# Thirty edge-list transfers moved into the drain of each middle convolution, out of the groups of the relational pass

## The reference, cut to what matters

```python
x = _layernorm(x + _L0(x, edge_index, ...))        # five attention convolutions, 4 heads
x = _layernorm(x + _L1(x, edge_index, types, ...)) # relational attention, 4 edge types
x = _layernorm(x + _L2(x, edge_index, ...))        # two GCN layers over (src, dst)
x = _layernorm(x + _L3(x, src, dst, weight, ...))  # out[src] += weight * h[dst]
```

## Time and profile before

| | |
|---|---|
| median of 3 runs | 5815.96 us (5811.11 to 5824.28) |
| the profiled execution | 5819.82 us, of which its span 5817.9 us |
| busy: PE, DVE, ACT, POOL | 3599.2, 3391.6, 1515.3, 4067.9 us |
| granted clock of PE, mean of the span | 0.686 |
| DMA, mean over the span | 117 GB/s |
| chain that ended last | no engine or line with as much as 1% of the span |
| edge passes of the middle convolutions, from POOL's first to its last gather | 747.9 to 1280.5, 1376.2 to 1908.5, 2005.5 to 2537.8 us |
| relational edge pass, POOL's first gather to its last transfer | 3345.7 to 4113.9 us |

### The profile page before, as it was taken

One profiled execution on the slowest core, in us unless ns is written; L12 is line 12 of the kernel. 1 busy time (PEld: TensorE's weight loads), 2 busy tenths in 40 slices (PEclk: granted clock), 3 DMA queues, 4 the chain that ended last, 5 costly groups with the idle time before them and its releaser, 6 DMA issues. The chain is left out here.

```text
span 5817.9 us, 84345 instructions
## 1 busy us (share of the span) xinstructions
PE 3599.2 (62%) x17681; PEld 2904.7 (50%) x17903; DVE 3391.6 (58%) x9203; ACT 1515.3 (26%) x3581; POOL 4067.9 (70%) x4170
## 2 busy tenths in 40 slices
PE   5667766666676656675787556666644444446555
PEld 3556546654666456554565345656533333334334
DVE  7777756665666556665666366666444343336665
ACT  4334323432343333333454322222100010000000
POOL 4477577766777577757777677777577767766775
PEclk6777767867777777787898755555655555557877
DMA  7656365645565366636664342332122222212111
GB/s 236 171 170 184 84 205 171 189 124 165 170 184 166 106 192 181 175 87 202 174 181 120 88 86 65 67 73 46 38 53 52 53 62 53 52 48 57 52 52 51
DMA packets 632362, 681.70 MB, mean 117 GB/s; under 512 B 179026, under 2 KB 514488, under 8 KB 631800
## 3 DMA queue, kind: packets, MB, share of 16 engines
q0 software_dynamic: 166560, 384.79, 24.1%
q1 hardware_dynamic: 465496, 293.65, 17.6%
HBM read 620.51 MB, written 57.47 MB: 117 GB/s over the span
## 5 line engine op out<-in xcount | busy, mean ns | idle before, releaser
L616 POOL DMA_INDIRECT kvconv<-kv_tab,src_all x1664 | 1626.4, 977 | 648.7 <-issue 497.8
L616 POOL DMA_INDIRECT rowsg_<-h_tab,src_all x832 | 788.7, 948 | 319.8 <-issue 253.0
L630 POOL DMA_INDIRECT lst_tab<-pay,ord_now x416 | 428.3, 1029 | 315.8 <-issue 244.7
L616 POOL DMA_INDIRECT rowss_<-h_tab,dst_i_g x416 | 399.1, 959 | 160.4 <-issue 120.1
L616 POOL DMA_INDIRECT rows_r<-rel_tab,idx_r x416 | 412.6, 992 | 132.7 <-issue 125.0
L616 POOL DMA_INDIRECT kvlast<-kv_tab,src_all x416 | 409.9, 985 | 133.1 <-issue 122.2
L1057 ACT ACTIVATE Sconv<-s8conv 128x512 f32<-128x512 fp8e4 x384 | 240.7, 627 | 401.3 <-PE pA1conv L1015 286.4
L1119 DVE TENSOR_TENSOR msgconv<-kvconv,sm_attEconv 128x512 f32<-128x512 f32 x416 | 285.6, 687 | 78.3 <-PE pA0conv L1015 28.0
L1015 PEld LDWEIGHTS pA0conv<-Sconv,msgconv 128*128 128x128 f32 x1664 | 303.0, 256 | 13.4
L1015 PE MATMUL pA0conv<-Sconv,msgconv 128*128 128x128 f32 x1664 | 302.0, 342 | 10.6 <-issue 6.5
L1015 PEld LDWEIGHTS pA1conv<-Sconv,msgconv 128*128 128x128 f32 x1664 | 291.4, 247 | 17.0
(11 more groups left out here) (681 smaller groups left out, 8861.6 us busy)
## 6 DMA issues: line engine op xcount, KB each, us to landing
qwinconv<-q_tab SPq DMA_DIRECT2D x1664, 64.0 KB
kvconv<-kv_tab,src_all POOLq DMA_INDIRECT x1664
st8conv<-st_tab SPq DMA_DIRECT2D x52, 512.0 KB
s8conv<-s_tab SPq DMA_DIRECT2D x52, 512.0 KB
qwinlast<-q_tab SPq DMA_DIRECT2D x416, 64.0 KB
kv_tab<-stageconv_n SPq DMA_DIRECT2D x28, 512.0 KB, 3.2
rowsg_<-h_tab,src_all POOLq DMA_INDIRECT x832
rel_tab<-stage_r SPq DMA_DIRECT2D x28, 272.0 KB, 3.9
```

The costliest lines, as they stand in the source:

```text
L616: nc.gpsimd.indirect_dma_start(rows[:, par * TG + t, :], None, tab, bass.IndirectOffsetOnAxis(ap=idx[:, g * TG + t:g * TG + t + 1], axis=0 ...
L630: nc.gpsimd.indirect_dma_start(lst_tab, bass.IndirectOffsetOnAxis(ap=ord_now[:, i:i + 1], axis=0), pay[:, i, :], None).then_inc(sem("liste ...
```

## The change

The batch of a middle convolution grows from 34 to 64 columns. `fetch` loads all 64; POOL issues the first 30 behind the 416 gathers of that convolution's edge pass, and the other 34 in the joint as before, where it waits for the landing of all. In the relational pass two transfers follow each group in place of ten, all 26 from one load by SP, so that the load in mid-pass goes, and the last batch there grows from 40 to 54. Joint 0, the last convolution, the stage behind it and the projection stage keep theirs. The total stays 416.

```diff
@@ -37,8 +37,9 @@
 RW = D + 2 * H
 JOINT = 34
 DRAIN = 30
-EACH = 10
-LISTED = [(CONVS - 1) * JOINT, DRAIN + 32, 48, EACH * GROUPS, 40]
+PER = DRAIN + JOINT
+EACH = 2
+LISTED = [JOINT + 3 * PER, DRAIN + 32, 48, EACH * GROUPS, 54]
 MOST = 70
 assert sum(LISTED) == T
 NT = NPAD // P
@@ -762,8 +763,8 @@
                 def _(pool):
                     pool.wait_ge(sem("ord_in"), 32 * (l + 1))
                     settle(pool)
-                    list_rows(pool, JOINT)
-                    pool.wait_ge(sem("listed"), 16 * JOINT * (l + 1))
+                    list_rows(pool, JOINT, 0 if isinstance(l, int) else DRAIN)
+                    pool.wait_ge(sem("listed"), 16 * PER * l + 16 * JOINT)
                     settle(pool)
 
                 @block.sync
@@ -918,8 +919,10 @@
                 @block.gpsimd
                 def _(pool):
                     gather_all(pool, lambda g, par: gather_group(pool, tag, l, g, par, kv_tab, src_all, kv), since)
-                    if deg is not None:
-                        pool.wait_ge(sem("ord_in"), 32 * CONVS)
+                    if rank is None:
+                        pool.wait_ge(sem("ord_in"), 32 * (l + 1))
+                        if not isinstance(l, int):
+                            settle(pool)
                         list_rows(pool, DRAIN)
 
                 @block.sync
@@ -1369,7 +1372,7 @@
 
                 def fetch(sp):
                     if not first:
-                        order_in(sp, l * JOINT, JOINT)
+                        order_in(sp, l * PER - DRAIN, PER)
                     load_next(sp, l + 1, nx)
                     sp.dma_start(nx["ln"][:, :], col0[ds(l, 1), :, :].rearrange("l p n -> (l p) n")
                                  ).then_inc(sem("nx_cols"), 16)
@@ -1557,16 +1560,11 @@
                         gather_group(pool, tag, 0, g, par, rel_tab, idx1, rows)
                         if g == 0:
                             pool.wait_ge(sem("ord_in"), 32 * (CONVS + 2))
-                        if g == 6:
-                            pool.wait_ge(sem("ord_pool"), 32)
-                        list_rows(pool, EACH, EACH * (g if g < 6 else g - 6))
-                        if g == 5:
-                            pool.wait_ge(sem("listed"), 16 * (sum(LISTED[:3]) + 6 * EACH))
-                            order_in(pool, sum(LISTED[:3]) + 6 * EACH, 7 * EACH, "ord_pool")
+                        list_rows(pool, EACH, EACH * g)
                     gather_all(pool, group)
                     pool.wait_ge(sem("listed"), 16 * sum(LISTED[:4]))
                     order_in(pool, sum(LISTED[:4]), LISTED[4], "ord_pool")
-                    pool.wait_ge(sem("ord_pool"), 64)
+                    pool.wait_ge(sem("ord_pool"), 32)
                     list_rows(pool, LISTED[4])
                     pool.wait_ge(sem("listed"), 16 * T)
 
@@ -1599,7 +1597,7 @@
                                     settle(sp)
                                 scatter_rows(g + 1, 1 - par)
                     scatter_rows(0, 0)
-                    order_in(sp, sum(LISTED[:3]), 6 * EACH)
+                    order_in(sp, sum(LISTED[:3]), LISTED[3])
                     for g in range(3):
                         group(g, g % 2)
                     with sp.Fori(1, (GROUPS - 1) // 2 - 1) as k:
```

## The result

The changed kernel takes 5829.87 us (median of 13 runs), the kernel before 5814.51 us in the 13 runs beside it: a ratio of 1.0026, 95% interval 1.0019 to 1.0034, 15.4 us slower. One of the changed kernel's 13 runs was a slow one (5917.82 us, at a mean granted clock of 0.602 where the others have 0.68 to 0.69) and stands outside the ratio. The forecast was 5839 us.

What follows compares the result with a forecast made beforehand. A ring of DVE softmax and PE sums was taken to pace the relational pass, POOL's DRAIN the edge-pass ends; +28.4 + 3 - 4.5 - 4 = +22.9 us on the profiled 5819.8 gave 5842.7, stated as 5839, range 5822 to 5856.

Steps and rivals of the forecast that it cites:

- three middle drains: Ends of the three middle edge passes: 30 more list transfers make POOL end late, 9.4 to 9.5 us each, +28.4.
- joints, forecast from PE's lower clock: Joints behind the middle passes: PE idles, then starts at its lower clock; 0 to 3.2 us each, taken as +3 together.
- relational end: End of the relational pass: POOL's DRAIN no longer holds the block, despite 14 more transfers; -4.5 us, bounds 0 and 4.5.
- late rows: Relational groups: DVE's waits for gathered rows at L1783 go; 4 us gained, bounds 0 and 33.
- POOL's own 34 transfers start and end as before: Joints behind the middle passes: POOL's list transfers there keep their times, counted from the block's start.
- The free DRAIN: Rival at the middle drains: the DRAIN is free or overlaps and hides the transfers; -7.6 us, 5808, chance 0.13.
- The released clock: Rival in the relational pass: PE's clock rises to 2.4 GHz with POOL off its limit; -108 us, 5731, chance 0.06.
- the ring: Relational pass: DVE softmax and PE sums alternate and set the pace, about 54.4 us a group; POOL runs beside it.
- Cold joints: Rival: PE's clock stays low through three joints, some 10 us more each instead of 1; 5866 us, chance 0.05.

Runs made afterwards that it cites:

- fifth experiment: Changed kernel with 22 list transfers per middle drain instead of 30, four per relational group, 52 behind the last; 5804.31 us against 5813.71 for the kernel before, ratio 0.9983.
- tenth experiment: Changed kernel with 22 transfers per middle drain, 26 per joint, 40 in projection, seven per relational group, 53 behind; 5785.95 us against 5813.82 for the kernel before.
- the spread list: Changed kernel with 22 transfers per middle drain, fewer in joints and projection, seven per relational group; against the kernel before 0.9952, in slower runs 1.0018 and 1.0023.

## Why the prediction was right, and where it was off

The forecast of slower by over 0.2% came true, and the time fell into the forecast's own range; it lay 9 us under the number given. Every term had the right sign and the largest had the right size.

| step | forecast | changed kernel's trace |
|---|---|---|
| three middle drains | +28.4 | +28.1 (10.8, 8.7, 8.6) |
| joints, forecast from PE's lower clock | +3 | +3.2 (1.5, 0.5, 1.2), by POOL's wait |
| relational end | -4.5 | -4.4 (POOL's DRAIN no longer last) |
| late rows | -4 | -8.6 (7.7 between the turns, 0.9 behind the last) |
| sum | +22.9 | +18.3 |

**The drains.** The price came from the same sequence in the last convolution, and it held: 9.05 us from the last transfer to the DRAIN's end in all three where 9.1 was taken. Counted from the last gather the EVENT comes 10.3, 10.0 and 9.4 us later than before (9.4 to 9.5 forecast), 29.6 together; the gathers themselves took 1.5 us less in sum, which is what brings the passes to 28.1. The fifth experiment confirms it from the other side, by taking away 8 of the 30.

**The joints.** The size was right, and that is in part luck: the way was another. PE's clock fell as said, and SP came 1.6 us later; but "POOL's own 34 transfers start and end as before" missed the wait behind them. They took 45.9 us as before, and their landing came 3.8 us after the last one in each joint, where it had taken 2.3, 3.4 and 2.7: +1.5, +0.4, +1.1, nearly the three joints' own differences. In the fifth experiment, whose joints start at clock 1.00, that landing took 3.2, 3.2 and 2.8 us and the joints 53.3, 53.1 and 52.2, together 1.2 us more than before. So a landing can be later by most of a microsecond without the lower clock, and by this comparison some 2.0 us of the 3.2 go with it. Whether SP's later stores delay the landing was not tried.

**The relational end.** POOL's DRAIN was to end 8 us ahead of ACT's; it ended 5.6 ahead, which is enough. The 14 more transfers cost nothing; the tenth experiment, where 53 behind groups of seven were two too many, shows how near the limit lies.

**The late rows** are the term that was mis-sized: "-4 ... 1.07 at the last group, 0.26 at the fifth, and an estimate of 2.6 for DVE work pushed back". The view of waits had 22.9 us of it, and I took the one period I had looked into (54.61) for all of them. Of the two that cost, 58.09 and 57.14, the longer begins at 3607.38, a turn that stands in the earlier trace rows, but its distance to the next was not taken. A list of all twelve intervals would have shown them. The whole pass had 38.8 us of these waits, not the 33 taken as the upper bound. The pause at the loop's turn, which makes a wait of 3.6 to 4.8 us cost 2.7 to 3.7, was not in the forecast at all.

**What is left.** By these terms the profiled executions should differ by 18.3 us, and the medians by that; they differ by 10.1 and 15.4. The profiled pair holds -4.5 us ahead of the first middle gather and -3.5 in the last convolution to the projection stage, where neither kernel differs. The fifth experiment's profile has the first of these too (743.8) and not the second (715.3 for 715.5). The gathers that fill most of the first convolution start at 198.4 us before, 194.7 in the changed kernel, 195.7 in the fifth experiment and 198.5 in the tenth, in a part of the program where no kernel differs. So both may be scatter between executions; this was not tested, and 3 us between the terms and the medians stay unexplained.

**The rivals.** The free DRAIN fell: the changed kernel's first DRAIN of 25.9 us ends 9.0 us behind the last transfer, and the EVENT behind that. The Trainium skill (VectorE: DVE Perf Modes, The DRAIN you can't avoid) gives its 12 ns on all five engines for the DRAINs of a program's preamble and postamble. Taken for a block's end as well, it would have given this rival's 5808 us; POOL's DRAINs at the ends of blocks with indirect transfers took 2.2 us or more in every trace here, those of blocks without them 0.04 (L723) to 0.49 (L143, both in the kernel before). The released clock fell: the periods stay at 54.4 with two, four and seven transfers a group, while POOL waits, and the granted clock stays at 0.50 from 3560 to 4000 us in the changed kernel; so the ring and not GpSimd paced the pass, in this kind of run. Cold joints fell: 53.6 us, not 62.

## What to carry to other kernels

Where the profile shows other engines working on beside it, work on a queue-issuing engine at a block's end is free up to the moment when the others are through, and from there each piece costs its full length: here 39.1 us of cover hold 6.9 + 1.38 n (the DRAIN's end after the last gather, for n transfers), so 22 transfers cost nothing and 30 cost 9 to 10 us, three times. Look in every stage for who ends last and by how much before deciding how many to put where; the projection stage gave 10.8 us for eight transfers, more than the whole relational pass did for its late rows. And where a loop has a steady period, list all of its periods: the mean wait said 2.5 us a group, while the loss sat in two groups out of twelve.

## What the runs showed of the hardware that was not expected

- **POOL's DRAIN at a block's end** costs 0.083 us for each list transfer in a block that holds these alone and waits for their landing: 2.17 us for 26, 2.66 for 32, 2.825 for 34, 3.32 for 40, 3.97 for 48. Straight behind unlanded ones it ends 6.6 us after the last of 416 gathers, and 8.4 us (22 list transfers behind the gathers) to 9.05 us (30) after the last. Gathers don't count like this, and the sum does not hold for the relational pass: its DRAIN took 9.0 to 9.3 us, with 80 to 170 list transfers beside 416 gathers.
- **A hardware loop's turn** stands with a pause of DVE of 2.8 to 3.1 us each time, three times in the relational pass, in both kernels and in the fifth and tenth experiment. Its cause is not shown; it cost time only behind late rows.
- **A second kind of run**, 30% longer, in which the other engines nearly stand still while GpSimd issues list transfers in a drain, for about 1.2 us each; beside gathers they go on. There the schedules that hide transfers gained nothing, and only fewer transfers helped. The same edit (the spread list) was worth -28 us in one kind of run and +11 to +15 in the other, and a trace shows which kind it is by TensorE's idle time without a reason: under 60 us, or over 1500.
